# Window attention with a frequency gate on one core: projection rows two at a time, one addition for both, exponentials ahead of the output copy, one normalising instruction

## The chip, the cores and the metric

The kernel runs on one core of one Trainium2 chip. The metric is the device time of one execution in microseconds (us). Five engines work side by side: PE (TensorE, matmuls and transposes; its weight loads are listed apart as PEld), DVE (VectorE), ACT (ScalarE), POOL (GpSimd) and SP (SyncE, which only issues transfers here). Each runs its own instructions in order and waits on semaphores for the others.

## The reference, cut to what matters

`x` is 8 images of 256 channels and 96x96 pixels, all float32. Every 12x12 window is attended to with 8 heads of 32 channels; a depthwise 3x3 convolution ("lpe") times a noise mask is added to the projected result.

```
win  = windows of x, 144 tokens each (8 x 8 windows in an image)
q, k, v = win @ qkv_w.T + qkv_b                       # 8 heads of 32
attn = softmax(q k^T / sqrt(32) + bias)               # 144 x 144 for each head and window
out  = attn @ v;  out = out @ proj_w.T + proj_b       # back to the image
x_lpe = (depthwise_conv3x3(x) + lpe_b) * lpe_scale * noise_mask
freq2 = dct2(out_image + x_lpe)
x_freq = idct2(freq2 * sigmoid(5 * (|freq2| - mean(freq2))))
y = gelu(batchnorm(conv1x1(x + x_freq)))
```

The noise mask comes from a DCT of `x` and is computed before the attention.

## The kernel before, in words

One program does three things after one another: the noise mask of all images (to about 830 us), then for each of the 8 images the attention ("strip part", some 666 us) and the frequency and 1x1 part (some 340 us), and at the end batch norm and gelu.

The strip part walks over 8 strips of 12 pixel rows. A strip is 16 steps: step t takes half of the heads of one window (4 window pairs, 2 windows, 2 groups of four heads). `each_strip` emits strip 0 (`head=True`), a loop whose body holds two inner strips and runs three times, and strip 7 (`last=True`). All four engines have a hand-written order for a step t:

- PE (L1150 on): the scores of t+3 for four heads (`score`, results in PSUM banks 0 to 3, one head in each), a first piece of q, k or v (`piece`, every step), the transposes of t (`transposes`, L1085 to L1088), then in some steps one row of the strip before (`row`), then second pieces (`made[1:]`, in even steps only), the attention of t-1 (`attend`), the small transposes of t, `attend_few(t-1)`, whose end raises `av`, and `few_scores(t+4)`.
- DVE: `pt_out(t-1)` (L779, L781), `scores_out(t+3)` (five instructions, L766), then two or three (in the last three steps of strip 7: six) `lpe_step`s (L797, L802, taps of the convolution), with `row_masked` (L812) after the first and `row_added` (L818) after the second in steps that have a row, `recip(t+2)` (L773), and the remaining `lpe_step`s.
- ACT: `o_out(t-2)` (L572, copies the attention's output out of its one PSUM bank, waits for `av`), `exps(t+2)` (five exponentials, L556), `piece_out` (L542, L545, L550), `pt_out(t)` (L564).
- POOL: `normalise(t+1)`: one TENSOR_TENSOR of 80 elements for the rest tokens (L433), then five TENSOR_SCALARs of 128 elements (L437), one for each column block. `transposes` waits for it. Now and then `windows` (L425).

A row is 96 pixels by 256 channels: PE transposes the lpe row (L1133) and projects the attention row with `wproj`, both into one PSUM bank; `row_masked` makes mask * lpe + bias in `rowt`, `row_added` adds the projection and writes it into `A`, whose layout is (channel, row): the 256 results of a row lie 96 elements apart. Rows go in steps 2 to 7 and 10 to 15 (`row_at`), one in each, through bank 3 (`psRow`). So the scores of the following step may write head 3 only once `a_row` tells that the addition has read the bank. In the last strip twelve more rows follow at the end, through banks 0 to 3 in turn.

Of the kernel before, what the change touches and what calls it, by code (L numbers as in the profile page):

```python
# [68 lines left out]
def build(nc, a, out, B):  # L69
# [6 lines left out]
    with ExitStack() as ctx:  # L76
# [59 lines left out]
        rowt = [carve("a", C) for _ in range(2)]  # L136
# [45 lines left out]
        psRow = 3  # L182
# [46 lines left out]
        def row_at(t):  # L229

            return t - 2 if 2 <= t < 8 else t - 4 if t >= 10 else None

        def rows_before(t):

            return sum(row_at(i) is not None for i in range(t))
# [137 lines left out]
        def _(g):  # L373
# [39 lines left out]
            with g.Fori(0, B) as b:  # L413
                def strip(s, par, head=False, last=False, first=False):
# [16 lines left out]
                    def normalise(t):  # L431
# [4 lines left out]
                        for c in range(LC):  # L436
                            o = g.tensor_scalar(sp[t % 4][:, c, L - 128:L], sp[t % 4][:, c, L - 128:L],  # L437
                                                rden[t % 4][:, c:c + 1], None, ALU.mult)
                        o.then_inc(S["norm_done"], 1)
# [45 lines left out]
        def _(act):  # L485
# [43 lines left out]
            with act.Fori(0, B) as b:  # L529
                def strip(s, par, head=False, last=False, first=False):  # L530
# [54 lines left out]
                    for t in range(NT):  # L585
                        if not (head and t < 2):
                            o_out(t - 2)
                        if not (last and t + 2 >= NT):
                            exps(t + 2)
# [72 lines left out]
        def _(v):  # L662
# [92 lines left out]
            with v.Fori(0, B) as b:  # L755
                def strip(s, par, head=False, last=False, first=False):
# [63 lines left out]

                    def mask_rows(y):

                        v.tensor_copy(mrow[0:96], mask[:, bass.ds(b, 1), bass.ds(y, WS)]
                                      .rearrange("p b h -> p (b h)")).then_inc(S["mrow_ready"], 1)
# [8 lines left out]
                    for t in range(NT):  # L833
# [8 lines left out]
                        r = None if head else row_at(t)  # L842
                        for half, k in steps[:1]:
                            lpe_step(half, k)
                        if r is not None:
                            row_masked(n - 1, r, psRow)
                        for half, k in steps[1:2]:
                            lpe_step(half, k)
                        if r is not None:
                            row_added(n - 1, r, psRow, s * WS - WS + r)  # L850
# [97 lines left out]
        def _(pe):  # L948
# [75 lines left out]
            with pe.Fori(0, B) as b:  # L1024
                def strip(s, par, head=False, last=False, first=False):
# [42 lines left out]
                    def score(t, rows=None, signal=True):  # L1068

                        p, v, hg = t // 4, t // 2 % 2, t % 2  # L1070
                        for j in range(HG):
                            if j == psRow and rows is not None:
# [81 lines left out]
                    for t in range(NT):  # L1154
# [8 lines left out]
                        r = None if head else row_at(t)  # L1163
                        if r is not None:
                            if not (last and t + 3 >= NT):
                                pe.wait_ge(S["sb_ready"], n * 80 + LC * (t + 3) + psRow + 1)
                            pe.wait_ge(S["a_row"], (n - 1) * WS + r + 1)
                            row(n - 1, r, psRow, 1 - par)
# [130 lines left out]
```

## Time and profile before

| | before |
|---|---|
| median of 3 runs | 9218.36 us (9204.33 to 9221.74) |
| profiled execution | 9222.4 us, its span 9220.8 us |
| mean granted TensorE clock | 0.931 of full speed |
| PE busy | 8240.3 us (89% of the span) |
| DVE busy | 5469.2 us (59%) |
| ACT busy | 5129.6 us (56%) |
| POOL busy | 4772.7 us (52%) |

Read it as follows. Busy time of an engine is the union of its instructions. A row of the timeline gives the start, the time from there to the end of the last of the instructions merged in it, the engine, the line, the operation, the operands' shapes and, in brackets, how long the engine had been idle and whose end released it. L950 is the helper that issues all matmuls, so its rows are told apart by shape: 128x144 with 128*32 weights is `attend`, 16x144 and 32x144 are the few rows and the scores, 128x288, 128x256 with 128x64 are the pieces, and 128x256 with `wproj` is a row. The first matmul of `transposes` (L1085) comes once in each step; the time from one of them to the next is called a frame here, and frame t starts with the transposes of step t.

### The profile page before, as it was taken

How to read it: one execution, taken by the hardware profiler on the slowest of the kernel's cores; microseconds unless marked ns; L12 is line 12 of the kernel's file. 1: busy time of each engine (PE TensorE's matmuls, PEld its weight loads, DVE VectorE, ACT ScalarE, POOL GpSimd, SP SyncE). 2: the span in 40 equal slices, each digit the busy share in tenths (PEclk: the TensorE clock that was granted, in tenths of full speed). 3: DMA queues.
4: the chain of work that ended last, by engine and by line, in shares of the span. 5: the costliest groups of instructions: out<-in, count | busy, mean ns of one | idle time of the engine just before them, and what ended most of it. 6: DMA issues, size and time to landing. Idle time of an engine off the chain costs nothing. (4 is left out here: it accounts for less than half of the span.)

```text
span 9220.8 us, 265192 instructions
## 1 busy us (share of the span) xinstructions
PE 8240.3 (89%) x88874; PEld 6129.4 (66%) x88874; DVE 5469.2 (59%) x20355; ACT 5129.6 (56%) x16576; POOL 4772.7 (52%) x7513
## 2 busy tenths in 40 slices
PE   9998998999998999999898999899999989899930
PEld 8996666766676666666685667666666668566720
DVE  4554776467745775377646774477537774577410
ACT  5555664366644664366546664466436654666434
POOL 1112775177724774277616772477427762677300
PEclk9998998999989998999999998999899999999875
DMA  7551000200012000200020000200020002000089
GB/s 126 97 99 34 21 14 21 83 14 15 14 36 67 15 20 15 83 15 20 21 78 14 21 14 30 68 20 20 15 83 15 20 21 72 19 21 14 13 318 409
DMA packets 386950, 487.51 MB, mean 53 GB/s; under 512 B 249616, under 2 KB 352528, under 8 KB 369296
## 3 DMA queue, kind: packets, MB, share of 16 engines
q1 hardware_dynamic: 369488, 393.67, 14.9%
q0 software_dynamic: 16192, 77.49, 2.1%
q8 instruction: 726, 11.89, 0.6%
q14 instruction: 544, 4.46, 0.2%
HBM read 319.45 MB, written 151.66 MB: 51 GB/s over the span
## 5 line engine op out<-in xcount | busy, mean ns | idle before, releaser
L437 POOL TENSOR_SCALAR work<-work 128x128 f32<-128x128 f32 x5120 | 3575.3, 715 | 0.0
L950 PE MATMUL ps<-work 128*32 128x144 f32 (+4 forms) x32902 | 1823.7, 302 | 304.4 <-ACT work L545 89.3
L556 ACT ACTIVATE work<-work 128x144 f32<-128x144 f32 x5120 | 2043.4, 403 | 0.9
L802 DVE SCALAR_TENSOR_TENSOR work<-xs,lw,work 128x570 f32<-128x570 f32 (+1 forms) x2048 | 1655.1, 819 | 0.0
L950 PEld LDWEIGHTS ps<-work 128*32 128x32 f32 (+3 forms) x32902 | 1012.3, 127 | 905.9 <-issue 564.6
L766 DVE CUSTOM_DVE_ANT_0 work<-ps,negbias 128x144 f32<-128x144 f32 x5120 | 1247.2, 303 | 615.0 <-issue 431.0
L950 PE MATMUL ps<-work,wqkv 128*128 128x288 f32 x4096 | 1317.0, 446 | 109.1 <-POOL work L449 78.1
L433 POOL TENSOR_TENSOR work<-work 128x80 f32<-128x80 f32 x1024 | 437.5, 427 | 1345.9 <-DVE work L773 1338.6
L468 POOL TENSOR_TENSOR work<-work 96x384 f32<-96x384 f32 x512 | 421.0, 822 | 1109.8 <-DVE work L874 1109.8
L950 PEld LDWEIGHTS ps<-work,wqkv 128*128 128x128 f32 x4096 | 733.3, 197 | 393.8 <-POOL work L425 82.5
L556 ACT ACTIVATION_READ_ACCUMULATOR work<-work 128x1 f32 x5120 | 970.8, 190 | 0.0
L572 ACT ACTIVATE work<-ps,qb 128x144 f32<-128x144 f32 x1024 | 389.6, 380 | 826.2 <-PE ps L950 818.5
L950 PE MATMUL ps<-dct,AH 96*96 96x97 f32 (+1 forms) x7168 | 822.0, 269 | 9.7 <-ACT AH L491 9.2
L950 PE MATMUL ps<-wproj,work 128*96 128x256 f32 x3072 | 824.7, 393 | 0.0
L950 PEld LDWEIGHTS ps<-dct,AH 96*96 96x96 f32 (+1 forms) x7168 | 774.8, 185 | 13.0 <-ACT AH L491 11.8
L812 DVE SCALAR_TENSOR_TENSOR work<-ps,work,pb 96x256 f32<-96x256 f32 x768 | 368.6, 480 | 697.1 <-PE ps L950 697.1
L950 PE MATMUL ps<-wqkv,work 128*32 128x64 f32 (+1 forms) x10240 | 753.3, 261 | 4.5 <-ACT work L550 4.5
L564 ACT ACTIVATE work<-ps 128x512 f32<-128x512 f32 x1024 | 603.2, 589 | 225.3 <-PE ps L1088 225.3
L950 PE MATMUL ps<-inv,work 96*96 96x96 f32 (+1 forms) x5632 | 702.3, 271 | 13.9 <-DVE work L880 8.7
L950 PEld LDWEIGHTS ps<-wqkv,work 128*32 128x32 f32 (+1 forms) x10240 | 509.2, 126 | 267.4 <-issue 176.8
L950 PEld LDWEIGHTS ps<-inv,work 96*96 96x96 f32 (+1 forms) x5632 | 631.4, 183 | 65.5 <-DVE work L880 11.3
L425 POOL COPY work<-xs 128x288 f32<-128x288 f32 x512 | 212.5, 444 | 869.9 <-issue 840.8
(126 smaller groups left out, 12080.5 us busy)
## 6 DMA issues: line engine op xcount, KB each, us to landing
work<-in_x SPq DMA_DIRECT2D x128, 576.0 KB, 5.5
xs<-in_x SPq DMA_DIRECT2D x64, 1152.0 KB, 5.3
AH<-in_x SPq DMA_DIRECT2D x192, 384.0 KB, 3.4
y_scratch<-AH SPq DMA_DIRECT2D x192, 384.0 KB, 2.5
AH<-y_scratch SPq DMA_DIRECT2D x64, 1152.0 KB, 23.4
out<-AH POOLq DMA_DIRECT2D x64, 1152.0 KB, 17.7
xs<-in_x SPq DMA_DIRECT2D x112, 96.0 KB, 5.0
bias_scratch<-in_rpb_rev POOLq DMA_DIRECT2D x144, 4.5 KB, 2.1
```

The source lines that it names most:

```text
L425: last = g.tensor_copy(xw[p % 2][:, ct, 0:2 * L].rearrange("p (v h w) -> p v h w", v=2, w=WS), src[:, ct, 1:WS + 1, 2 * WS * (p % NP):2 * ...
L433: g.tensor_tensor(rest[t % 4][:, :, 0:L - 128], sp[t % 4][:, :, 0:L - 128], rden[t % 4].unsqueeze(2).broadcast_to([128, LC, L - 128]), ALU ...
L437: o = g.tensor_scalar(sp[t % 4][:, c, L - 128:L], sp[t % 4][:, c, L - 128:L], rden[t % 4][:, c:c + 1], None, ALU.mult)
L468: g.tensor_tensor(tg[par][0:96], tg[par][0:96], msb[par][0:96].unsqueeze(2).broadcast_to([96, 4, 96]), ALU.subtract).then_inc(S["tg_ready" ...
L556: o = act.activation(sp[t % 4][:, c, :], sp[t % 4][:, c, :], ACT.Exp, scale=-1.0, bias=mn[t % 4][:, c:c + 1], accum_out=den[t % 4][:, c:c ...
L564: act.activation(pt[t % 2][:, 0:HG, 0:128], psT, ACT.Copy).then_inc(S["pt_a"], 1)
L572: act.activation(ostrip[side][:, hg, :, w0:w0 + WS], psO.rearrange("p (h w) -> p h w", w=WS), ACT.Identity, bias=qb[:, 4 + hg:5 + hg]).the ...
L766: v.tensor_tensor_reduce(out=sp[t % 4][:, c, :], in0=psS[c], in1=negbias[:, t % 2, c, :], scale=1.0, scalar=BIG, op0=ALU.add, op1=ALU.min, ...
L802: v.scalar_tensor_tensor(dst[:, ct, :, w0:w1], xs[side][:, ct, y0 + dy:y0 + dy + HS, w0 + dx - 1:w1 + dx - 1], lw[:, ct, tap:tap + 1], dst ...
L812: v.scalar_tensor_tensor(rowt[r % 2][0:96], ps[0:96, bank, C:2 * C], mrow[0:96, r:r + 1], pb[:], ALU.mult, ALU.add).then_inc(S["row_mask"], 1)
L950: return nc.tensor.matmul(o, l, r, start=start, stop=stop)
```

## The change

It does four things.

1. `row_at` gives two rows in each of the steps 3, 5, 7, 11, 13 and 15, and none in the others. The even one goes through bank 2, the odd one through bank 3. PE waits once for both banks, the score of the next step waits for `a_row` at head 2 in place of head 3.
2. DVE does both `lpe_step`s first, then two `row_masked`, then one `rows_added`, which reads the two banks and the two halves of `rowt2` element by element in turn and writes both rows: 256 runs of two neighbouring elements, 96 elements apart.
3. ACT does `exps(t+2)` ahead of `o_out(t-2)`.
4. POOL's five TENSOR_SCALARs become one TENSOR_TENSOR of 5x128 elements with the reciprocals broadcast.

The rows at the end of the last strip stay single.

```diff
-        rowt = [carve("a", C) for _ in range(2)]
+        rowt2 = carve("a", 2, C)
+        rowt = [rowt2[:, i] for i in range(2)]
...
-        psRow = 3
+        psRow = (2, 3)
...
-            return t - 2 if 2 <= t < 8 else t - 4 if t >= 10 else None
+            return list(range(t - 3, t - 1)) if t in (3, 5, 7) else list(range(t - 5, t - 3)) if t in (11, 13, 15) else []
...
-                        for c in range(LC):
-                            o = g.tensor_scalar(sp[t % 4][:, c, L - 128:L], sp[t % 4][:, c, L - 128:L],
-                                                rden[t % 4][:, c:c + 1], None, ALU.mult)
-                        o.then_inc(S["norm_done"], 1)
+                        g.tensor_tensor(sp[t % 4][:, :, L - 128:L], sp[t % 4][:, :, L - 128:L],
+                                        rden[t % 4].unsqueeze(2).broadcast_to([128, LC, 128]),
+                                        ALU.mult).then_inc(S["norm_done"], 1)
...
+                        if not (last and t + 2 >= NT):
+                            exps(t + 2)
                         if not (head and t < 2):
                             o_out(t - 2)
-                        if not (last and t + 2 >= NT):
-                            exps(t + 2)
...
+                    def rows_added(m, r, y):
+
+                        v.wait_ge(S["row_mask"], m * WS + r + 2)
+                        v.tensor_tensor(A[:, :, bass.ds(y, 2)],
+                                        ps[0:96, psRow[0]:psRow[0] + 2, 0:C].rearrange("p h c -> p c h"),
+                                        rowt2[0:96].rearrange("p h c -> p c h"), ALU.add).then_inc(S["a_row"], 2)
...
-                        r = None if head else row_at(t)
-                        for half, k in steps[:1]:
+                        rows = [] if head else row_at(t)
+                        for half, k in steps[:2]:
                             lpe_step(half, k)
-                        if r is not None:
-                            row_masked(n - 1, r, psRow)
-                        for half, k in steps[1:2]:
-                            lpe_step(half, k)
-                        if r is not None:
-                            row_added(n - 1, r, psRow, s * WS - WS + r)
+                        for r in rows:
+                            row_masked(n - 1, r, psRow[r % 2])
+                        if rows:
+                            rows_added(n - 1, rows[0], s * WS - WS + rows[0])
...
-                            if j == psRow and rows is not None:
+                            if j == psRow[0] and rows is not None:
                                 pe.wait_ge(S["a_row"], rows)
...
-                        r = None if head else row_at(t)
-                        if r is not None:
+                        rows = [] if head else row_at(t)
+                        if rows:
                             if not (last and t + 3 >= NT):
-                                pe.wait_ge(S["sb_ready"], n * 80 + LC * (t + 3) + psRow + 1)
-                            pe.wait_ge(S["a_row"], (n - 1) * WS + r + 1)
-                            row(n - 1, r, psRow, 1 - par)
+                                pe.wait_ge(S["sb_ready"], n * 80 + LC * (t + 3) + psRow[1] + 1)
+                            pe.wait_ge(S["a_row"], (n - 1) * WS + rows[0] + 1)
+                        for r in rows:
+                            row(n - 1, r, psRow[r % 2], 1 - par)
```

## Rows read from the trace of the kernel before

**Rows 1.** Busy time by stretch: the strip part of image 1 (length, engines, clock).

```profile
1874.00:2540.00 666.00, 621.52 (x8004) 432.51 (x8004) 489.10 (x2075) 442.97 (x1687) 512.55 (x816) 0.98 0.05 15
```

**Rows 2.** Timeline of PE, head strip of image 2, frames 10 to 13, no rows.

```profile
2924.00 0.33 PE L1085 MATMUL ps<-eye,work 128*128 128x128 f32 x1
...
2928.74 0.27 PE L1085 MATMUL ps<-eye,work 128*128 128x128 f32 x1
...
2929.49 0.45 PE L950 MATMUL ps<-work 128*32 128x144 f32 x8
...
2931.02 1.24 PE L950 MATMUL ps<-work,wqkv 128*128 128x288 f32 x4
2932.09 0.27 PE L1085 MATMUL ps<-eye,work 128*128 128x128 f32 x1
...
2933.26 1.24 PE L950 MATMUL ps<-work,wqkv 128*128 128x288 f32 x4 [0.35 <-ACT work L545]
...
2935.95 1.24 PE L950 MATMUL ps<-work,wqkv 128*128 128x288 f32 x4
2937.03 0.27 PE L1085 MATMUL ps<-eye,work 128*128 128x128 f32 x1
...
2938.60 0.45 PE L950 MATMUL ps<-work 128*32 128x144 f32 x8 [0.76 <-ACT work L545]
...
2941.55 0.33 PE L1085 MATMUL ps<-eye,work 128*128 128x128 f32 x1
```

**Rows 3.** Timeline of PE, an inner strip of image 2, frames 2 to 5, one row each.

```profile
3130.58 0.33 PE L1085 MATMUL ps<-eye,work 128*128 128x128 f32 x1
...
3136.26 0.27 PE L1085 MATMUL ps<-eye,work 128*128 128x128 f32 x1
...
3141.47 0.27 PE L1085 MATMUL ps<-eye,work 128*128 128x128 f32 x1
...
3146.88 0.27 PE L1085 MATMUL ps<-eye,work 128*128 128x128 f32 x1
...
3152.43 0.33 PE L1085 MATMUL ps<-eye,work 128*128 128x128 f32 x1
```

**Rows 4.** Timeline of all engines, inside frame 3 of that strip.

```profile
3138.20 0.48 DVE L812 SCALAR_TENSOR_TENSOR work<-ps,work,pb 96x256 f32<-96x256 f32 x1 [0.80 <-PE ps L950]
...
3139.32 0.58 DVE L818 TENSOR_TENSOR AH<-ps,work 96x256 f32 x1
...
3140.40 1.24 PE L950 MATMUL ps<-work,wqkv 128*128 128x288 f32 x4
```

**Rows 5.** Timeline of PE, rows back to back at the end of image 2.

```profile
3564.34 0.38 PE L1133 MATMUL ps<-eye,work 128*96 128x128 f32 x2
...
3565.42 0.38 PE L1133 MATMUL ps<-eye,work 128*96 128x128 f32 x2
```

**Rows 6.** Groups by line and shape: count, busy us, mean ns of one.

```profile
L437 POOL TENSOR_SCALAR work<-work 128x128 f32<-128x128 f32 x5120 | 3575.3, 715 | 0.0
...
L468 POOL TENSOR_TENSOR work<-work 96x384 f32<-96x384 f32 x512 | 421.0, 822 | 1109.8 <-DVE work L874 1109.8
...
L818 DVE TENSOR_TENSOR AH<-ps,work 96x256 f32 x576 | 339.2, 589 | 0.0
...
L880 DVE TENSOR_TENSOR work<-ps,work 96x384 f32<-96x384 f32 x512 | 278.7, 544 | 12.6 <-ACT work L614 12.6
...
L897 DVE TENSOR_TENSOR AH<-ps,AH 128x768 f32<-128x768 f32 x192 | 181.0, 943 | 54.3 <-PE ps L950 53.7 <-DMA AH<-in_x 0.6
```

**Rows 7.** Timeline of ACT, head strip of image 2, the copy of piece k=3, frame 13.

```profile
2937.65 0.48 ACT L545 ACTIVATE work<-ps,qb 128x288 f32<-128x288 f32 x1
```

**Rows 8.** Timeline of PE, last strip of image 2, frames 13 and 15 begin.

```profile
3529.53 0.45 PE L1085 MATMUL ps<-eye,work 128*128 128x128 f32 x1 [3.24 <-POOL work L437]
...
3546.82 0.45 PE L1085 MATMUL ps<-eye,work 128*128 128x128 f32 x1 [4.07 <-DVE work L781]
```

**Rows 9.** Timeline of POOL, last strip of image 2, steps of one normalise.

```profile
3523.57 5.72 POOL L437 TENSOR_SCALAR work<-work 128x128 f32<-128x128 f32 x5
```

More of the change, by code:

```diff
@@ L229, in row_at @@
         def row_at(t):
-            return t - 2 if 2 <= t < 8 else t - 4 if t >= 10 else None
+            return list(range(t - 3, t - 1)) if t in (3, 5, 7) else list(range(t - 5, t - 3)) if t in (11, 13, 15) else []
         def rows_before(t):
-            return sum(row_at(i) is not None for i in range(t))
+            return sum(len(row_at(i)) for i in range(t))
         def taps_at(t, head, last):
```

## The prediction

> **What bounds the kernel now.** I read the busy time by stretch first. In the strip part of an image PE is busy 621.5 of 666.0 us at a granted clock of 0.98, DVE 489, POOL 513, ACT 443 [rows 1]. The stretch is bound by PE's order, and what can be won are the places where PE stands in it. The change touches only this part; eight strip parts are 58% of the profiled span. Then I read the timeline of PE by frames (from one L1085 matmul to the next), first where no rows run, then where each step has one, because the difference prices a row and shows what a wait costs.
>
> Without rows, frames 10 to 13 take 4.74, 3.35, 4.94 and 4.52 us [rows 2]. Two stalls are in them, both released by ACT's piece copy (L545). In frame 11, where nothing holds PE, the work behind the transposes starts 0.75 us after the frame's start. In frame 12 (the second piece) it starts 1.17 in, in frame 13 (`attend`) 1.57. So unstalled frames would be 4.74, 3.35, 4.52 and 3.70.
>
> With one row each, frames 2 to 5 take 5.68, 5.21, 5.41 and 5.55 [rows 3]. A row costs PE 1.08 us, the distance of rows back to back [rows 5]. Frame 3 then has 5.21 - 3.35 - 1.08 = 0.78 us too much, and frame 5 likewise 5.55 - 3.70 - 1.08 = 0.77. That is the score of the next step waiting at head 3 for `row_added`: L818 ends at 3139.90, and the next piece starts 0.50 later [rows 4]. Frames 2 and 4 have a second piece between row and scores, and there the same wait is covered (0.94 and 0.89 us more than without a row).
>
> **The change part by part.** *Even frames lose their row.* Frames 2, 6, 10, 14 fall from 5.68 to 4.74, frames 4 and 12 from 5.41 to 4.52: 4 x 0.94 + 2 x 0.89 = 5.54 us in a strip [rows 2, 3]. Frames 0 and 8 never had one.
>
> *Odd frames get two.* On PE: frames 3, 7, 11, 15 become 3.35 + 2.16 + S = 5.51 + S, frames 5 and 13 become 3.70 + 2.16 + S = 5.86 + S, where S is the new stall at the scores. Against 5.21 and 5.55 that costs 4 x 0.30 + 2 x 0.31 = 1.82, and 6 S in a strip.
>
> *The size of S.* In frame 3 the first `row_masked` starts 1.94 us in, when its row is ready, and takes 0.48 [rows 4]. The second row is ready 1.08 later, at 3.02, so the second `row_masked` ends at 3.50 and the addition starts at about 3.54. The two `lpe_step`s ahead are done by then: they stand in the 1.5 us in which DVE waits for the rows. The addition takes D. After it PE needs the 0.50 seen now, and about 0.10 more since head 2 too has to follow (my estimate). Without a row the next piece starts at 2.28 (2931.02 after 2928.74, [rows 2]), so with two and no stall at 2.28 + 2.16 = 4.44. So S = 3.54 + D + 0.60 - 4.44 = D - 0.30. Queued behind the addition on DVE are `recip`, the third `lpe_step` and `pt_out`; the next frame has no row and takes that up.
>
> *D is the unknown.* No instruction of before writes runs of two or reads two banks in turn. Dense additions from PSUM take 544 ns for 384 elements and 943 for 768, 1.04 ns an element [rows 6]; so 256 would take 411 ns and 512 take 0.68 us: the lower end. L818 writes 256 lone elements and takes 589, that is 178 ns more than 411. Paid for every element again, D is 2 x 589 = 1.18: the upper end if reads cost nothing extra. Paid for each run, as a new place is opened 256 times either way, D is 0.68 + 0.18 = 0.86. I take that, as the number of runs stays as in L818's row, and S = 0.56. The Trainium skill ("SBUF — State Buffer", Door 1: The DMA port swizzle) says that full bandwidth needs at least two hits in a 16-byte line. By it the runs of two would be written free and D would be 0.68; it would also count against the reads, which come from a new line each time. L818's surcharge over a dense write fits that sentence; the runs of two are what no row shows.
>
> *Exponentials ahead of the output copy.* In frame 13 the piece that ACT must copy ends on PE at 2937.19, but the copy (L545) starts at 2937.65, since five exponentials are in front, which themselves waited behind `o_out` for `av` [rows 2, 7]. With the exponentials first, ACT does them in that idle time and the copy starts at about 2937.24 and ends 0.41 earlier. The release to `attend` now takes 2938.60 - 2938.13 = 0.47. Frame 13 would be some 0.39 shorter: 4.13 instead of 4.52; its like are frames 1 and 9 in every strip and 5 and 13 in a head strip. Frame 12 of a head strip loses about 0.33 of its 0.42. In frames with rows, ACT has no part in the stall. What is now later is `o_out(t-2)`, and `attend(t-1)` waits for it. By ACT's order it ends about 0.35 us into the frame and `attend` starts at 0.75, later with rows, so I price that at nothing; if ACT were full, each frame would lose some tenths.
>
> *One normalising instruction.* Five of 715 ns become one [rows 6]. For 640 elements, L468's 822 ns for 384 bounds it at 822 x 640/384 = 1.37 us. POOL drops from 3.6 us a step to under 1.4, off PE's path: in inner strips `norm_done` comes long before the transposes. Worth nothing there. In the last strip it is worth something: PE waits 3.24 us for L437 before frame 13, as POOL needed 5.72 us for five TENSOR_SCALARs while DVE ran `lpe_step` after `lpe_step` [rows 8, 9]; and 4.07 for DVE's `pt_out` before frame 15. There rows one at a time also made DVE idle for the row in step 14, which now has none. I estimate 5 us for each last strip (the 3.24 most of all, and some 3 from step 14, less about 1 for the longer rows of step 15), with 2 and 8 as bounds.
>
> **The sum.** An inner strip: 5.54 + 2 x 0.39 - 1.82 - 6 x 0.56 = 1.14 us less; 48 of them: 55. A last strip: steps 0 to 9 give 2 x 0.94 + 0.89 + 0.78 - 0.91 - 3 x 0.56 = 0.96, and 5 at the end: 8 x 6.0 = 48. A head strip has no rows: 3 x 0.33 + 3 x 0.39 = 2.2; 8 of them: 18. Together 121 us. The profiled execution took 9222.4, which gives 9101; the median is 4 us below it, which gives 9097. I say 9097.
>
> S enters 6 x 48 + 3 x 8 + 3 x 8 = 336 times. D = 0.68 gives 9037, D = 1.18 gives 9204. The last strips' bounds add 24 either way.
>
> **The rivals.**
> - *Runs of two are written free* (D = 0.68): 9037. For it speaks that dense writes run at full rate; against it that nothing here writes pairs.
> - *Every element pays, or reads pay in part* (D from 1.0 to 1.2): 9144 to 9211. L818's row is for it if the surcharge is for elements and not for places.
> - *Slower: the addition pays for its interleaved reads as well.* The two inputs change bank and half with each element. If writes pay 0.36 and one read 0.36, D is 1.40 and the time 9097 + 0.54 x 336 = 9278. It decides from D = 1.22 on, where nothing is left of the 121 us. Against it: nothing in the trace shows a read that costs more than a dense one.
> - *The new order on ACT brings nothing*, because `o_out` is late for `attend` as often as the copy is early. Then 0.78 x 56 + 18 = 62 us are missing: 9159.
> - *POOL's one long instruction gets in DVE's way.* POOL and DVE's `lpe_step` hinder each other, since five TENSOR_SCALARs took 5.72 us beside it and 715 ns on average each [rows 6, 9]. An instruction of 1.37 us started just before an `lpe_step` in a frame with rows would delay the masks by what the 0.6 us of slack there don't cover, some 0.7 us: up to +235 us. But `recip` releases POOL after the rows, and the next frame is one without rows. The Trainium skill ("SBUF — State Buffer", Who interferes with whom) says that the two engines take a shared port for a whole instruction, when DVE has two SBUF inputs; the stretched TENSOR_SCALARs agree with it.
>
> **How the numbers follow.** Forecast (D from 0.77 to 1.0, 9065 to 9145): 45%. Written free: 18%. D from 1.0 to 1.2: 15%. ACT's order brings nothing: 8%. Slower by the reads: 11%, by POOL: 3%. The range 9010 to 9210 takes in both ends of D and most of the last strips' bounds; it leaves out the slower cases and a little at the low end. A measurement of this kernel can tell about 0.2% from no change (18 us). Faster by more: 82%; within: 6%; slower: 12%.
>
> **What would show it.** Mean duration of the pair addition: 0.86 us (0.68 or 1.18 or more decides between the rivals). Frames without rows at 4.74 and 4.52, frames 1 and 9 at 4.13, frames 3 and 5 at 6.07 and 6.42 with PE released by the addition. L545 no longer a releaser in head strips. A single TENSOR_TENSOR of at most 1.4 us on POOL, and no wait for it in the last strip. Wrong I would be if DVE reached the masks late in row frames, or if `attend` waited for `o_out`.

## The result, and the profile after

The changed kernel takes 8996.88 us (median of 4 runs, 8976.02 to 9006.15); the kernel before took 9214.2 beside it (9204.33 to 9221.74). The ratio is 0.9762, with a 95% interval from 0.9741 to 0.9783: faster by 217 us, where 121 were forecast and 9010 was the low end of the range. The profiled execution took 8990.8 us (span 8989.2, mean granted clock 0.940), against 9222.4 before: 232 us less.

The page of after, busy time of the engines. POOL has lost 2146 us and DVE 62, PE only 101, though the span lost 232:

```profile
PE 8138.9 (91%) x88874; PEld 6060.7 (67%) x88874; DVE 5407.6 (60%) x20019; ACT 5172.7 (58%) x16576; POOL 2627.1 (29%) x3417
```

Groups by line and shape of after (count, busy us, mean ns of one, idle before). L824 is the pair addition, L818 the single one that is left, L437 the new normalising instruction:

```profile
L437 POOL TENSOR_TENSOR work<-work 128x640 f32<-128x640 f32 x1024 | 1297.2, 1267 | 0.0
...
L824 DVE TENSOR_TENSOR AH<-ps,work 96x512 f32 x288 | 199.3, 692 | 50.5 <-DVE work L812 12.0
L818 DVE TENSOR_TENSOR AH<-ps,work 96x256 f32<-96x256 f32 x96 | 57.5, 599 | 3.3
```

PE of after, an inner strip of image 2, frames 3 to 5 (the transposes' first matmul is L1090 now), and the piece that follows the scores in frame 3, to be read beside [rows 3]. Frame 3 takes 5.91 us where it took 5.21, frame 4 4.52 where it took 5.41, frame 5 6.26 where it took 5.55:

```profile
3060.93 0.27 PE L1090 MATMUL ps<-eye,work 128*128 128x128 f32 x1
...
3061.81 1.03 PE L955 MATMUL ps<-wproj,work 128*96 128x256 f32 x4
...
3062.89 1.03 PE L955 MATMUL ps<-wproj,work 128*96 128x256 f32 x4
...
3065.76 1.24 PE L955 MATMUL ps<-work,wqkv 128*128 128x288 f32 x4
3066.84 0.27 PE L1090 MATMUL ps<-eye,work 128*128 128x128 f32 x1
...
3071.36 0.27 PE L1090 MATMUL ps<-eye,work 128*128 128x128 f32 x1
...
3077.62 0.33 PE L1090 MATMUL ps<-eye,work 128*128 128x128 f32 x1
```

DVE inside frame 3, beside [rows 4]. The second mask waits 0.60 us for its row, the pair addition starts 3.64 us into the frame and ends at 4.33, and the piece above starts 0.50 after that:

```profile
3062.87 0.48 DVE L812 SCALAR_TENSOR_TENSOR work<-ps,work,pb 96x256 f32<-96x256 f32 x1
3063.95 0.48 DVE L812 SCALAR_TENSOR_TENSOR work<-ps,work,pb 96x256 f32<-96x256 f32 x1 [0.60 <-PE ps L955]
3064.57 0.69 DVE L824 TENSOR_TENSOR AH<-ps,work 96x512 f32 x1
```

PE of after, head strip of image 2, frames 11 to 13 (3.35, 4.56, 4.12 us, where [rows 2] has 3.35, 4.94, 4.52):

```profile
2860.61 0.27 PE L1090 MATMUL ps<-eye,work 128*128 128x128 f32 x1
2863.96 0.27 PE L1090 MATMUL ps<-eye,work 128*128 128x128 f32 x1
2868.52 0.27 PE L1090 MATMUL ps<-eye,work 128*128 128x128 f32 x1
2872.64 0.33 PE L1090 MATMUL ps<-eye,work 128*128 128x128 f32 x1
```

**Where the time went.** Cut the span at the strip parts and at the frequency part (from its first DCT matmul to the first 1x1 matmul), and sum each over the 8 images. The strip parts went from 5327.4 to 5149.0 us, 178 less. The frequency parts, which the change does not touch, went from 1337.8 to 1287.5, 50 less. The rest, 3 us. These are figures of one execution of each kernel: that of before lies 8 us above its median and that of after 6 below, so some 15 of the 232 us, and with them perhaps part of the 50, come from which executions were profiled. The strip parts are steadier: 5321.6 and 5324.7 in e11 and e14, whose strips are those of before, 5146.4 and 5149.2 in e8 and e12, whose strips are those of after. So a difference of up to 6 us in them means nothing. Busy time by stretch, image 2, first its strip part and then its frequency part (length, PE, PEld, DVE, ACT, POOL, granted clock, DMA share, GB/s); of before:

```profile
2880.88:3546.82 665.94, 621.49 (x8004) 432.52 (x8005) 489.19 (x2075) 442.90 (x1687) 516.37 (x818) 0.98 0.05 15
3574.73:3745.74 171.01, 168.56 (x1312) 142.98 (x1313) 70.73 (x193) 90.39 (x193) 52.63 (x64) 0.86 0.08 24
```

and of after:

```profile
2814.71:3458.78 644.07, 616.84 (x7998) 429.04 (x7999) 482.21 (x2033) 448.22 (x1687) 249.85 (x313) 0.98 0.05 15
3485.86:3648.47 162.61, 158.76 (x1313) 135.60 (x1313) 70.69 (x193) 90.37 (x193) 52.64 (x64) 0.92 0.08 25
```

The frequency part does the same work in both; what differs is the granted clock, 0.86 against 0.92.

### The profile page after: what moved, and what is told of

Read it like the earlier page. It is cut to its first block, busy times and chain, and to the rows that moved or that the text cites. A ratio compares the mean times of both kernels' runs of the same rounds, so it can differ in the third digit from the quotient of the medians.

```text
span 8989.2 us, 259528 instructions
## 1 busy us (share of the span) xinstructions
PE 8138.9 (91%) x88874; PEld 6060.7 (67%) x88874; DVE 5407.6 (60%) x20019; ACT 5172.7 (58%) x16576; POOL 2627.1 (29%) x3417
## 3 DMA queue, kind: packets, MB, share of 16 engines
q14 instruction: 528, 4.33, 0.2%
## 4 chain that ended last, share of the span: by engine, by line
issue 49%; POOL 24%; PE 20%; DMA 4%; POOLq 1%; DVE 1%; ACT 1%; SPq 0%; DVEq 0%
PE ps L955 20%; POOL work L437 13%; POOL work L434 5%; POOL work L426 3%; POOL work L468 3%; DMA AH<-y_scratch 2%; DMA out<-AH 1%; POOLq L465 0%; POOLq L433 0%; PE ps L1138 0%; ACT AH L657 0%; DVE work L802 0%; POOLq L216 0%; DVE work L674 0%; DVE work L907 0%
## 5 line engine op out<-in xcount | busy, mean ns | idle before, releaser
L955 PE MATMUL ps<-work 128*32 128x144 f32 (+4 forms) x32902 | 1782.2, 301 | 170.9 <-issue 96.9
L802 DVE SCALAR_TENSOR_TENSOR work<-xs,lw,work 128x570 f32<-128x570 f32 (+1 forms) x2048 | 1594.6, 815 | 0.0
L434 POOL TENSOR_TENSOR work<-work 128x80 f32<-128x80 f32 x1024 | 538.4, 526 | 3350.2 <-DVE work L773 3350.2
L437 POOL TENSOR_TENSOR work<-work 128x640 f32<-128x640 f32 x1024 | 1297.2, 1267 | 0.0
L955 PE MATMUL ps<-dct,AH 96*96 96x97 f32 (+1 forms) x7168 | 800.1, 264 | 9.7 <-ACT AH L491 9.2
L955 PEld LDWEIGHTS ps<-dct,AH 96*96 96x96 f32 (+1 forms) x7168 | 753.5, 181 | 13.0 <-ACT AH L491 11.8
L955 PEld LDWEIGHTS ps<-wqkv,work 128*32 128x32 f32 (+1 forms) x10240 | 490.7, 126 | 246.3 <-issue 176.5
L1093 PE MATMUL ps<-eye,work 128*128 128x128 f32 x4096 | 630.3, 278 | 0.0
L955 PE MATMUL ps<-AH,work 128*128 128x384 f32 (+2 forms) x2188 | 621.8, 521 | 7.8 <-DVE work L725 4.7
L639 ACT ACTIVATE AH<-ps 128x768 f32<-128x768 f32 x192 | 155.8, 811 | 732.5 <-PE ps L955 732.5
```

Source lines behind the costliest of these rows:

```text
L434: g.tensor_tensor(rest[t % 4][:, :, 0:L - 128], sp[t % 4][:, :, 0:L - 128], rden[t % 4].unsqueeze(2).broadcast_to([128, LC, L - 128]), ALU ...
L437: g.tensor_tensor(sp[t % 4][:, :, L - 128:L], sp[t % 4][:, :, L - 128:L], rden[t % 4].unsqueeze(2).broadcast_to([128, LC, 128]), ALU.mult) ...
L639: act.activation(ys[par], ps[:, 4 + 2 * par:6 + 2 * par, 0:384], ACT.Copy).then_inc(S["y_ready"], 1)
L802: v.scalar_tensor_tensor(dst[:, ct, :, w0:w1], xs[side][:, ct, y0 + dy:y0 + dy + HS, w0 + dx - 1:w1 + dx - 1], lw[:, ct, tap:tap + 1], dst ...
L955: return nc.tensor.matmul(o, l, r, start=start, stop=stop)
L1093: last = nc.tensor.transpose(psT[:, j, :], sp[t % 4][:, j, L - 128:L], eye[:])
```

## The experiments

Figures of "strip parts" and "frequency parts" below are sums over 8 images in the profiled execution, to be read against 5327.4 and 1337.8 of before and 5149.0 and 1287.5 of after. Each is of one execution; a kernel's frequency parts differ between executions far more than its strip parts. None of these kernels leaves work out; some add some.

**Rows in pairs alone (e1_rows_only).** The changed kernel with ACT's order and the five TENSOR_SCALARs of before:

```diff
-                        if not (last and t + 2 >= NT):
-                            exps(t + 2)
                         if not (head and t < 2):
                             o_out(t - 2)
+                        if not (last and t + 2 >= NT):
+                            exps(t + 2)
...
-                        g.tensor_tensor(sp[t % 4][:, :, L - 128:L], ...)
+                        for c in range(LC):
+                            o = g.tensor_scalar(sp[t % 4][:, c, L - 128:L], ...)
```

> The kernel before with the row part of the change alone (two rows in odd steps, one addition for both). Theory A, the parts of the change add up in the strip part and the frequency part only follows the clock it is left with: with the pair addition at 0.69 us as measured, an inner strip gains 5.54 - 1.82 - 6 x 0.39 = 1.4 us, all strips some 80 us; the frequency part may move by up to 8 us an image either way of the clock alone. Theory B, the gain comes from the parts together (rows need the new ACT order to pay): under 40 us in the strip parts.

9190.36 us, ratio 0.9975 (0.9959 to 0.9992). Strip parts 5287.7: 40 us less. An inner strip takes 84.18 us instead of 85.28, its frames 3 and 5 take 5.90 and 6.27, as in after (5.90 and 6.26). The 80 us expected by theory A are missed: an inner strip gained 1.1 of the 1.4 us, and the last strip became 1.7 us longer (87.13 against 85.45).

**The new order on ACT alone (e2_act_only).** The kernel before with `exps(t + 2)` ahead of `o_out(t - 2)`.

> The kernel before with the exponentials ahead of the output copy alone. Theory A: 0.4 us in each of frames 1 and 9 of 56 strips and 2.2 to 2.8 in each head strip, some 65 us in the strip parts, nothing in frames with a row. Theory B: next to nothing by itself, since the output copy is late for attend as often as the piece copy is early.

9129.53 us, ratio 0.9907 (0.9876 to 0.9938). Strip parts 5260.1: 67 us less. Frames 1 and 9 fell from 4.51 and 4.54 to 4.10 and 4.11, a head strip from 68.76 to 66.13.

**One normalising instruction alone (e3_norm_only).** The kernel before with the single TENSOR_TENSOR.

> The kernel before with the single normalising instruction alone. Theory A: off PE's path except in the last strips, where PE waited 3.24 us for POOL; 0 to 4 us an image, up to 30 us. Rival: with POOL's port free DVE's lpe steps get shorter (812 to 760 ns) and PE's waits for the row addition shrink by some 0.1 us in 12 steps of 56 strips, 60 us more.

9245.33 us, ratio 1.0029 (1.0008 to 1.005). Strip parts 5328.4, nothing. Its profiled execution is the slowest of ten, with frequency parts of 1363.2 us, 25 more than before; that, and not the strips, is most of what it loses. Alone the edit wins nothing in a last strip (86.6 us against 85.45): POOL is done sooner, but PE then waits for DVE's `pt_out`, 5.2 us before frame 14 where it waited 3.57.

The three alone give 40 + 67 + 0 = 107 us in the strip parts, together 178. The next two find the missing 71.

**All but the normalising instruction (e6_old_norm)**, and **all but the new order on ACT (e7_old_act)**: the changed kernel with one of the two edits undone.

> The changed kernel with the five normalising instructions of before. Theory A, normalising matters only in the last strips: inner and head strips as in the changed kernel, the last strip of an image 5 to 7 us longer, since DVE's six lpe steps in a row keep POOL's five instructions waiting; strip parts +45 us in all, about 9045 if the frequency part stays. Rival, it is worth nothing as when taken alone: 8997 within 10.

> The changed kernel with the output copy ahead of the exponentials again. Theory A: 0.4 us more in frames 1 and 9, 0.12 more in frames 2 and 10, 2.8 us in a head strip: strip parts +85 us, about 9080. Rival: only what the order brought alone, +67 us.

e6: 9045.49 us, ratio 0.9812 (0.9776 to 0.9849), strip parts 5187.7, that is 39 us more than after. Nearly all of it is in the last strips (86.06 us against 81.47), inner strips are the same (82.72 against 82.70). PE and POOL of e6 in the last strip of image 2 (L438 is L437's old form there):

```profile
3464.41 0.45 PE L1091 MATMUL ps<-eye,work 128*128 128x128 f32 x1 [4.66 <-POOL work L438]
...
3471.02 9.44 POOL L434 TENSOR_TENSOR work<-work 128x80 f32<-128x80 f32 x1 [3.67 <-DVE work L774]
...
3483.69 0.45 PE L1091 MATMUL ps<-eye,work 128*128 128x128 f32 x1 [6.49 <-POOL work L438]
```

The same place in after: the wait before frame 13 is 2.56 us, for DVE.

```profile
3441.58 0.45 PE L1090 MATMUL ps<-eye,work 128*128 128x128 f32 x1 [2.56 <-DVE work L781]
...
3443.31 1.91 PE L955 MATMUL ps<-wproj,work 128*96 128x256 f32 x4
3445.36 1.03 PE L955 MATMUL ps<-wproj,work 128*96 128x256 f32 x4
3451.17 0.30 PE L1090 MATMUL ps<-eye,work 128*128 128x128 f32 x1 [3.95 <-DVE work L781]
3458.78 0.45 PE L1090 MATMUL ps<-eye,work 128*128 128x128 f32 x1 [5.48 <-POOL work L437]
```

So the single instruction is worth 39 us once the rows come in pairs: before frame 13 PE waits 4.66 us for POOL's five, where the kernel before waited 3.24 [rows 8] and after waits 2.56 for DVE. e7: 9101.27 us, ratio 0.9866 (0.9834 to 0.9898), strip parts 5255.5: the order is worth 106 us beside the other two edits, 67 alone. An inner strip loses 1.54 us without it. Between rows and order 33 us come only together (e6's 139.7 less 40 and 67). Some 22 of them are 0.47 us in each of 48 inner strips. Half of that is frames 2 and 10, which without a row are 4.62 with the new order and 4.74 with the old one; the rest lies mostly where one strip meets the next (frames 15 and 0). Some 10 are in the last strips.

**Two lone additions in place of the pair's (e4_two_adds).** The schedule of after, with a single addition for each row:

```diff
-                        if rows:
-                            rows_added(n - 1, rows[0], s * WS - WS + rows[0])
+                        for r in rows:
+                            row_added(n - 1, r, psRow[r % 2], s * WS - WS + r)
```

> The changed kernel with two single additions of 0.59 us in place of the pair addition of 0.69. Theory A: PE is released 0.45 us later in each of 336 pair frames, so some 150 us slower than the changed kernel, about 9150, more than half of the whole gain. Rival: PE's release is covered by then, and the time stays within 40 us of the changed kernel.

9041.37 us, ratio 0.9806 (0.9771 to 0.9841), strip parts 5161.9: only 13 us more than after, where 150 were expected. Frames 3 and 5 are 6.02 and 6.37, that is 0.12 and 0.11 longer. DVE in its frame 3 (which starts at 2981.01):

```profile
2982.95 0.48 DVE L812 SCALAR_TENSOR_TENSOR work<-ps,work,pb 96x256 f32<-96x256 f32 x1
2984.03 0.48 DVE L812 SCALAR_TENSOR_TENSOR work<-ps,work,pb 96x256 f32<-96x256 f32 x1 [0.60 <-PE ps L955]
2984.43 1.03 DVE L818 TENSOR_TENSOR AH<-ps,work 96x256 f32 x2
```

The two additions take 1.03 us together, not 2 x 0.59, as the second begins before the first has ended. And they start 3.42 us into the frame, 0.22 sooner than the pair's, because the first needs only the first mask. They end at 4.45, the pair's at 4.33: that is the 0.12. In the strip parts the new instruction is thus a small part of the gain; leaving the other frames without a row is the large one. The whole kernel is 44 us slower than after, though the intervals of the two ratios overlap: of the 45 us between the profiled executions 12 lie in the frequency parts and 12 between the strip parts and these (229.9 us against 218.0), where both kernels have the same single additions. No run shows how much of that is the instruction's.

**The pair addition with lone writes (e5_lone_writes).** The same 512 elements, with the rows outside, so that every element is written 96 elements from the last, and both reads are dense:

```diff
-                        v.tensor_tensor(A[:, :, bass.ds(y, 2)],
-                                        ps[0:96, psRow[0]:psRow[0] + 2, 0:C].rearrange("p h c -> p c h"),
-                                        rowt2[0:96].rearrange("p h c -> p c h"), ALU.add)
+                        v.tensor_tensor(A[:, :, bass.ds(y, 2)].rearrange("p c h -> p h c"),
+                                        ps[0:96, psRow[0]:psRow[0] + 2, 0:C],
+                                        rowt2[0:96], ALU.add)
```

> The changed kernel with the pair addition walking row by row: reads dense, 512 lone elements written 96 elements apart, in one instruction. If lone writes cost 178 ns per 256 as in the row of the single addition, it takes 0.68 + 0.36 = 1.04 us and PE is released 0.35 us later in 336 frames: +118 us, about 9115. If the 178 ns are paid once in an instruction (a fixed latency at its end), it takes 0.86 and the time is about 9055. If neither, 0.69 and 8997.

9088.94 us, ratio 0.985 (0.9819 to 0.9881), strip parts 5240.5. By source line, first after, then e5 (duration of one in ns, min/median/max):

```profile
L824 DVE TENSOR_TENSOR AH<-ps,work x336: 687/692/697, 945.5 to 8337.7; 96x512 f32 x144, 96x512 f32<-96x512 f32 x24
```

```profile
L824 DVE TENSOR_TENSOR AH<-ps,work x336: 1010/1025/1041, 946.5 to 8464.4; 96x512 f32 x144, 96x512 f32<-96x512 f32 x24
```

333 ns more, about twice the 178 that L818 pays for 256 lone writes [rows 6]. The surcharge is for every element written alone, runs of two pay none of it, and interleaved reads pay nothing (0.692 us against the 0.68 of a dense addition of 512, worked out from [rows 6]). The difference of 0.33 us at 336 additions, 111 us at most, shows as 92 in the strip parts.

**The frequency part: start it 1.5 us later (e8_delay, e11_before_delay).** It begins when `image_done` is told. DVE's tick copy there is replaced by a long reduction, in after and in before. It only delays:

```diff
-                v.tensor_copy(tick[:, 2:3], tick[:, 3:4]).then_inc(S["image_done"], 1)
+                v.tensor_reduce(tick[:, 2:3], wqkv[:], AX.XY, ALU.max).then_inc(S["image_done"], 1)
```

> The changed kernel with DVE's last small copy before the frequency part of each image replaced by one long reduction, so that PE starts that part some 1.6 us later in each image and nothing else differs. Theory C, the frequency part's length is set by how long TensorE stays at the lower granted clock in it, which depends on when the part starts: its length moves to another of the values seen so far (156, 163, 165, 171 or 173 us), and the total differs from the changed kernel by far more or less than 8 x 1.6 = 13 us. Rival, the 8 us an image that the changed kernel gained there come from the change itself: the part stays at 162.6 us and the total is 13 us longer, 9010.

> The kernel before with the same late reduction as in the delayed version of the changed kernel: PE starts each frequency part some 1.6 us later. Theory C: the part, 171.0 us in five of eight images of before, moves to another of its values with the time at the lower clock, so the total differs clearly from 9218 + 13, either way. Rival: 9231.

e8: 8969.78 us, ratio 0.9736 (0.9703 to 0.9769). Its four executions took 8948.93, 8951.42, 8988.13 and 8989.99 us; the profiled one is the first, 42 us shorter than after's although each image waits 1.5 us more. Strip parts 5146.4, frequency parts 1234.2, all eight at 154.3 us. The other two executions were some 40 us longer, and the interval of e8's ratio overlaps that of after (0.9741 to 0.9783), so a gain by the delay isn't shown; that the frequency parts can take another length is. e11: 9222.02 us, ratio 1.0035 (1.0013 to 1.0058); its ten executions range from 9184.4 to 9279.83 us. In the profiled one, the fastest, the frequency parts took 154.3 to 174.6 us, 1289.5 in all. By the median the delay wins nothing in before.

How PE enters the frequency part of image 2; before, where the first sixteen matmuls run at the high clock level and those from 1.5 us on at the low one (1.60 us for the second row, which takes 0.89 in after):

```profile
3574.73 1.60 PE L950 MATMUL ps<-dct,AH 96*96 96x97 f32 x16
3576.22 1.60 PE L950 MATMUL ps<-work,dct 96*96 96x384 f32 x2
```

after, where it is high until 7.2 us into the part, some 0.8 us behind a wait of PE of 1.60 us; the matmuls from there on take 1.49 to 1.57 where they took 0.81 to 0.90:

```profile
3487.36 0.89 PE L955 MATMUL ps<-work,dct 96*96 96x384 f32 x2
...
3489.69 0.90 PE L955 MATMUL ps<-dct,AH 96*96 96x97 f32 x8
3492.18 0.86 PE L955 MATMUL ps<-work,dct 96*96 96x384 f32 x2 [1.60 <-DVE work L885]
...
3492.99 1.52 PE L955 MATMUL ps<-inv,work 96*96 96x96 f32 x8
3494.31 1.50 PE L955 MATMUL ps<-dct,AH 96*96 96x97 f32 x8
```

e8, where PE stands the same 1.60 us at the same place and the clock stays high:

```profile
3480.36 0.86 PE L955 MATMUL ps<-work,dct 96*96 96x384 f32 x2 [1.60 <-DVE work L885]
...
3481.16 0.90 PE L955 MATMUL ps<-inv,work 96*96 96x96 f32 x8
```

and ACT of after just before that wait, where it loads the table for the sigmoid:

```profile
3489.63 1.28 ACT L614 ACT_TABLE_LOAD   x1
```

**Load the table in time (e12_table_early, e13_table_fill, e14_before_table).** ACT's own tick, some 16 us ahead of the frequency part, becomes a sigmoid, so the table is loaded in idle time. e12 is after with it, e14 is before with it, e13 is e12 with four matmuls of filling on PE in each of the last three steps of the last strip. The edit that all three share:

```diff
-                act.activation(tick[:, 1:2], tick[:, 3:4], ACT.Copy).then_inc(S["image_done"], 1)
+                act.activation(tick[:, 1:2], tick[:, 3:4], ACT.Sigmoid).then_inc(S["image_done"], 1)
```

> The changed kernel with ACT's last small copy before the frequency part made a sigmoid, so that the 1.3 us load of the sigmoid table happens in ACT's idle time and not in front of the first gate, where PE waits 1.6 us. Theory D, that wait is what lets the clock fall at the start of the part: the time at the lower clock in it falls from 25 us to under 12 and its length from 162.6 to about 154 us in most images, 8 x 8 = 60 us in all, about 8935. Rival, the clock falls of the part's slow start itself: only the 1.3 us of the load are saved, 10 us, and the length still jumps with the start time.

> As before it, and four filler matmuls in steps 13 to 15 of the last strip: frame 13 of the last strip 1.9 us shorter as in the kernel with fillers, and the twelve rows behind it at the full clock, 4 us an image, 30 us in all beyond the kernel with the early table; the start time of the frequency part moves again, which under theory D no longer matters.

> The kernel before with the early table load alone. Theory D: its 171.0 us in five of eight images become 154 to 156, up to 100 us in all, about 9120. Rival: 9205, with lengths still between 154 and 173 us.

e12: 8921.89 us (8920.15 to 8937.22), ratio 0.9676 (0.9655 to 0.9698). Frequency parts 1214.7, all eight at 151.8 or 151.9; strip parts unchanged (5149.2). The table load has moved and PE's wait is 0.60 us:

```profile
3449.66 1.28 ACT L603 ACT_TABLE_LOAD   x1
```

```profile
3471.41 0.86 PE L955 MATMUL ps<-work,dct 96*96 96x384 f32 x2 [0.60 <-ACT work L609]
...
3472.21 0.90 PE L955 MATMUL ps<-inv,work 96*96 96x96 f32 x8
```

The stretch by windows:

```profile
3466.08:3617.88 151.80, 148.94 (x1312) 127.74 (x1313) 70.70 (x193) 89.22 (x192) 52.64 (x64) 0.98 0.09 27
```

e13: 8921.62 us, ratio 0.9672 (0.9652 to 0.9691), the same: the filling brings nothing. Its first matmuls stand behind the rows of step 13, so frame 13 stays at 9.76 us, and the 30 us expected were missed. e14: 9150.32 us, ratio 0.9923 (0.9898 to 0.9947), frequency parts 1284.4. Three images are at 151.8 or 151.9, four at 164.0, one at 173.0: in before the table is one cause of the low clock and not the only one. The granted clock tells them apart. In the profiled execution of before it falls 1.4 to 1.6 us into the part in five images, and PE has no wait of 1.60 us in them; in the other three PE has that wait and the clock falls at 7.2 to 7.9 us, as in all eight images of after. In e14 five images still fall at 1.3 to 1.6 us, and the other three don't fall at the start at all.

**Fill PE's waits in the last strip (e10_fill).** After with five such matmuls in each step from 12 on.

> The changed kernel with five matmuls of 256 columns into the unused bank 7 after the attention of steps 12 to 15 of the last strip, where PE waits for DVE. Theory C: PE is busy there, the granted clock falls later or not at all in those steps, the row projections of step 13 take 1.03 us instead of 1.9, so frame 13 of the last strip is 1 to 2 us shorter, 8 to 16 us in all, and the frequency part, starting at another time, has another length between 154 and 173 us. Rival: the clock there has another cause than PE's waiting; the frames stay at 9.7 and 7.6 us or grow by the fillers.

9002.46 us, ratio 0.9765 (0.9711 to 0.9819). PE in its last strip of image 2, with the filling ahead of frame 13 and the rows at 1.03 us each:

```profile
3437.68 4.11 PE L955 MATMUL ps<-wqkv,eye 128*128 128x256 f32 x10
3441.63 0.27 PE L1090 MATMUL ps<-eye,work 128*128 128x128 f32 x1
...
3442.51 1.03 PE L955 MATMUL ps<-wproj,work 128*96 128x256 f32 x4
```

Frame 13 fell from 9.73 to 7.76 us, frame 12 rose from 4.45 to 5.88, and the strip parts are 9 us shorter (5140.4), the stretches from there to the frequency parts 18 (199.8 against 218.0). But in this execution the frequency parts took 1334.8 us, at a granted clock of 0.86 in image 2: what was won before the stage was lost in it. The four executions range from 8943.02 to 9036.32 us, and the profiled one took 9026.55.

**Split the scores (e9_split).** After with the first piece put between heads 0, 1 and heads 2, 3 of the score that waits for `a_row`.

> The changed kernel with the next step's first piece moved between heads 0, 1 and heads 2, 3 of its scores, so that 1.06 us of PE's work stands in front of the wait for the pair addition. If the remaining 0.39 us a pair frame is that wait and nothing else, frames with rows fall from 5.90 to 5.51 and from 6.26 to 5.87, strip parts lose 0.39 x 330 = 130 us, total about 8870 with the frequency part as it was. Rival: DVE gets the scores 1.06 us later and its five score instructions become what the next frames wait for; nothing gained.

9004.98 us, ratio 0.9787 (0.9757 to 0.9817), strip parts 5150.6, no gain. PE at the end of its frame 3, the piece and then heads 2 and 3:

```profile
2981.57 1.24 PE L955 MATMUL ps<-work,wqkv 128*128 128x288 f32 x4
2982.74 0.51 PE L955 MATMUL ps<-work 32*128 32x144 f32 x4
2983.19 0.33 PE L1092 MATMUL ps<-eye,work 128*128 128x128 f32 x1
```

The scores of two heads (four matmuls in the row) take 0.51 us, those of four heads (eight) take 0.53 in a frame without a wait (2.99 to 3.52 us into frame 0 of after). Cutting the scores in two made frame 3 0.14 us longer (6.04) and frames 0 and 4 0.14 shorter (4.38), so the stall of 0.39 wasn't filled that way.

## Why the prediction was wrong

**The duration of the pair addition was the first wrong step.** "Paid for each run, as a new place is opened 256 times either way, D is 0.68 + 0.18 = 0.86. I take that": measured 0.692 (687 to 697) at every one of 336. I had turned "256 lone elements cost 178 ns more" into a price for places. e5 shows that it is a price for elements that have no neighbour: with lone writes 512 of them cost 333 ns, in runs of two nothing. The forecast's own terms carry the rest: 0.17 less, 336 times, is 57 us, so 178 us in place of 121. The strip parts lost 178.4. That would have been 9040 us, inside the range of 9010 to 9210; what took the result out of it is the second wrong step, the frequency parts, which the sum left as they were (below). For D this was the rival "written free" at 9037. The Trainium skill ("SBUF — State Buffer", Door 1: The DMA port swizzle) had it right for the writes: two hits in a 16-byte line are enough. For the reads its sentence would have asked for a price too, and 0.692 shows none.

**The size of S.** S = D - 0.30 held: 0.69 - 0.30 = 0.39, which gives 5.90 for frame 3 and 6.25 for frame 5, and the frames took 5.90 and 6.26 (frame 11, which the forecast had like frame 3, took 6.09). Inside, two errors of 0.10 us cancelled: the addition starts at 3.64, not 3.54, and PE follows it by 0.50, without the 0.10 that I added for head 2.

**The frames without rows.** Forecast 4.74 and 4.52; frames 4 and 12 are 4.52, frames 2, 6, 10 and 14 are 4.62 or 4.63. I had read frame 10 of before as free of stalls since no wait of PE is shown in it. It still held 0.12 us. In frames 2 and 10 that goes only with the new order on ACT (4.74 in e1, 4.62 in e6), in 6 and 14 with the paired rows (4.62 in e1). With 4 x 0.12 an inner strip comes to 2.16 + 0.48 = 2.64 us less; measured 2.58 (85.28 to 82.70).

**The order on ACT.** Right: frames 1 and 9 went from 4.51 and 4.54 to 4.10 and 4.09 (forecast 0.39 less), and nothing became late. e2 and e7 price it at 67 and 106 us, not at nothing as one rival had it. A head strip gained 2.8 us, not 2.2, again by frames 2 and their like.

**The last strips were over-valued.** Forecast 6 us each, or 7.0 with D of 0.69; measured 4.0 (15 frames, 85.45 to 81.47). Of that the first ten frames gave 1.7 and the end, frames 10 to 14, 2.2, where 5 were forecast between bounds of 2 and 8. Frames 12 and 14 lost their row (6.43 to 4.45, and 8.61 to 7.61), and PE's wait before frame 13 is 2.56 us for DVE where it was 3.24 for POOL [rows 8]. But frame 13 now has two rows and went from 8.56 to 9.73: its first row takes 1.91 us where others take 1.03, with the granted clock at its lower level. I had charged 1 us for longer rows and not the clock at which they run; in e10, with filling ahead of it, the row takes 1.03 and the frame 7.76.

POOL's single instruction took 1.27 us on average, but up to 2.30, where at most 1.4 was told, and its worth of 39 us is seen only beside paired rows. The sign "no wait for it in the last strip" failed: before frame 15 PE waits 4.71 to 5.54 us for L437 in all eight images (5.48 in image 2, above), where it waited for DVE before. The single instruction stood behind POOL's 80-element one (L434), which took 9.45 us there and ended at 3457.33, while DVE's `pt_out` had long been done:

```profile
3455.41 0.29 DVE L781 COPY work<-ps 128x144 f32<-128x144 f32 x1
```

In e4 the same 80-element instruction takes 0.81 us:

```profile
3456.26 0.81 POOL L434 TENSOR_TENSOR work<-work 128x80 f32<-128x80 f32 x1 [4.78 <-DVE work L773]
```

There frame 14 takes 4.68 us and not 7.61, but frame 13 takes 11.33 and not 9.73, and from the start of frame 13 to the frequency part before, after and e4 all take about the same, 44.8, 44.6 and 44.8 us on average. So the gain of the end lies in frames 10 to 12 (17.5 to 15.1 us), and of what bounds the rest no run shows more than the clock's part (e10: 40.4 us, for a frame 12 that is 1.4 longer).

The errors on the other strips (48 x 0.42 = 20 for inner ones, 5 for head strips, both too little gain) and this one (8 x 3.0 = 24, too much) cancel, which is why the sum above fits so exactly: that is luck.

**What the account left out.** "The change touches only this part" was true of the instructions and false of the time. The 50 us of the frequency parts are the second wrong step: the sum put them at nothing, because no edit touches them. In every profiled execution their length goes with the time that PE spent at the lower level (1.2 GHz) inside them, read from the records of the granted clock (in before's 171.0 us at a granted clock of 0.86, 46.6 us at half speed):

| frequency part, us | of it at the lower level, us | seen in |
|---|---|---|
| 151.8 | 4.6 to 4.8 | e12, all images |
| 154.3 | 8.5 | e8, all images |
| 155.9 | 12 | after, two images |
| 162.6 | 25.7 | after, six images |
| 171.0 | 46.6 | before, four images |
| 173.2 | 52 | e1, five images |

That the change gives 50 us there is no merit of its edits as they were meant: in the profiled executions a delay of 1.5 us takes another 53 off these parts (e8), and some filling in the last strip puts 47 back (e10). In after the loss starts behind the wait for the sigmoid's table in all eight images, and taking that wait away ends it (e12, whose four executions all lie between 8920.15 and 8937.22 us). The wait alone isn't enough: e8 has the same 1.60 us in all eight images and no fall of the clock behind it. **What stays open** is what else it takes, what makes the clock fall at 1.5 us in five images of before, and why two parts entered alike differ: images 0 and 5 of after have the same stretches of low clock in the 47 us before the part and the same fall at 7.2 us, and take 162.6 and 155.9 us. With the strip parts alone the forecast would have been 9040; the rest to 8997 is this part and the spread of the medians.

**A version that beats both.** e12 is 8921.89 us, 75 less than after, with one word of the program changed: a ratio of 0.9676 to before (0.9655 to 0.9698, clear of after's 0.9741 to 0.9783).

## What to carry to other kernels

Price a strided write by its lone elements: where results can be written in runs of two, the surcharge is gone, even if the reads are interleaved for it. Make a sum for the stages that are not edited as well: where a stage's granted clock differs between its repetitions in one trace, an edit before it can move its length by more than the edit itself is worth, and the figures of one execution don't tell what the edit did there. Look at each stage's first wait for a table load, and load the table in idle time before.

## What the runs showed of the hardware

- DVE writes of 4-byte elements 384 bytes apart cost 0.65 to 0.70 ns an element more (178 ns for 256, 333 for 512); in runs of two they cost nothing more, and reading two PSUM banks in turn with every element costs nothing either (0.692 us for 512).
- Two additions of 0.59 us, one behind the other on DVE, take 1.03 us together (e4): durations in the trace overlap, and their sum is an upper bound.
- POOL's 80-element TENSOR_TENSOR, 0.526 us on average, took 9.44 us beside DVE's chain of `lpe_step`s in e6, and 9.45 in after:

```profile
3447.88 9.45 POOL L434 TENSOR_TENSOR work<-work 128x80 f32<-128x80 f32 x1 [4.35 <-DVE work L773]
```

DVE at its beginning, four taps with two SBUF inputs each, and more behind them:

```profile
3447.73 2.95 DVE L802 SCALAR_TENSOR_TENSOR work<-xs,lw,work 128x570 f32<-128x570 f32 x4
```

The Trainium skill ("SBUF — State Buffer", Who interferes with whom) says that DVE, with two SBUF inputs, and POOL contend for a shared pair of ports, which one of them holds for a whole instruction while the other is blocked. The trace agrees that POOL is held up beside such work, 18 times its mean here. But its instruction runs beside more than one of DVE's, twelve taps of 0.8 us from 3447.73 to 3457.15, so POOL didn't get its turn after each; in e4 it did after one (0.81 us). No run shows what decides between the two.

- A table load of 1.28 us at the head of a stage cost 73 us in eight images (1287.5 against 1214.7), 9 us each: behind the wait for it the clock fell in all eight, for 3.4 or 20.5 us. In e8, with the same wait, it didn't fall.
